# Moving lookup-table work of VectorE and ScalarE one place forward in the attention loop of a perceiver kernel

## The reference, cut to what matters

```python
kvx = jnp.einsum('bsi,oi->bso', cond, w_kv_x)
kx, vx = jnp.split(kvx, 2, axis=-1)
kx = _ln(kx.reshape(b, sc, g, d), kxln_w, kxln_b)
vx = vx.reshape(b, sc, g, d)
xout = _gqa(qx, kx, vx).reshape(b, s, nh * d)
```

```python
def _ghost_linear(x, idx, lut):
    w = lut[idx]
    return jnp.einsum('bsh,oh->bso', x, w)
```

## Time and profile before

| | us |
|---|---|
| median of 3 runs | 427.55 |
| lowest, highest | 427.23, 427.74 |
| profiled execution | 427.4 |
| its span, first to last instruction | 425.6 |
| TensorE (PE) busy | 414.7 |
| VectorE (DVE) busy | 347.2 |
| ScalarE (ACT) busy | 248.8 |
| GpSimd (POOL) busy | 35.8 |

### The profile page before, as it was taken

The page is one execution under the profiler, slowest core; times in us unless marked ns, Lnnn a source line. Parts: engine busy times, 40 slices in busy tenths (PEclk is TensorE's granted clock), DMA queues, the critical chain, the costliest instruction groups (busy, mean ns, idle before and its releaser), DMA issues.

```text
span 425.6 us, 6868 instructions
## 1 busy us (share of the span) xinstructions
PE 414.7 (97%) x2427; PEld 292.2 (69%) x2433; DVE 347.2 (82%) x699; ACT 248.8 (58%) x780; POOL 35.8 (8%) x58
## 2 busy tenths in 40 slices
PE   8999999999999999999999999999999999999897
PEld 3453455788885767778676686785486799837596
DVE  5889999987999899689899998978887787746831
ACT  2478898688547777748986677664505263220220
POOL 0010000040000001100001000010010004101000
PEclk9999999999999999999999999999999999999999
DMA  7599120500002015993554835688337979730000
GB/s 240 226 191 415 39 85 2 199 2 26 27 2 99 1 51 123 201 306 78 132 124 92 198 70 108 155 187 359 74 78 246 390 267 241 151 125 2 2 2 25
DMA packets 14591, 56.80 MB, mean 133 GB/s; under 512 B 1824, under 2 KB 2912, under 8 KB 13280
## 3 DMA queue, kind: packets, MB, share of 16 engines
q1 hardware_dynamic: 11104, 39.31, 25.3%
q0 software_dynamic: 3456, 17.11, 21.4%
HBM read 41.40 MB, written 0.26 MB: 98 GB/s over the span
## 4 chain that ended last, share of the span: by engine, by line
PE 74%; DVE 12%; issue 6%; DMA 4%; ACT 3%; POOL 1%; SPq 0%; DVEq 0%; ACTq 0%; POOLq 0%
PE PS L482 11%; PE PS L1817 10%; PE PS L453 8%; PE PS L454 8%; PE PS L455 8%; PE PS L1846 3%; PE PS L535 3%; PE PS L1287 3%; DMA lutw_dt.float<-luttmp_dt.float 2%; PE PS L1832 2%; DMA raw_dt.float<-in_wk_nat 1%; PE PS L492 1%; PE PS L1153 1%; PE PS L1135 1%; PE PS L1295 1%
## 5 line engine op out<-in xcount | busy, mean ns | idle before, releaser
L605 ACT ACTIVATE sq_dt.float<-PS 128x128 bf16<-128x128 f32 x256 | 67.0, 279 | 27.0 <-PE PS L455 20.5
L482 PE MATMUL PS<-s_dt.float,ctx_ring_dt.float 128*128 128x512 f32 x128 | 57.8, 593 | 0.0
L605 ACT ACTIVATION_READ_ACCUMULATOR sq_dt.float<-PS 128x1 f32 x256 | 53.6, 210 | 0.0
L453 PE MATMUL PS<-wkc_dt.float32r,ctx_hi_dt.float32r 128*128 128x512 f32 x128 | 51.5, 402 | 0.1
L454 PE MATMUL PS<-wkT_dt.float32r,ctx_hi_dt.float32r 128*128 128x512 f32 x128 | 50.0, 390 | 0.0
L455 PE MATMUL PS<-wkc_dt.float32r,ctxT_ring_dt.float32r 128*128 128x512 f32 x128 | 49.9, 390 | 0.0
L687 ACT ACTIVATE luttmp_dt.float<-low_bit_dt.float,vec_dt.float,small_dt.float 128x1536 f32<-128x1536 uint8 x24 | 38.5, 1654 | 8.5 <-DMA lutw_dt.float<-luttmp_dt.float 8.5
L1817 PE MATMUL PS<-wch_dt.float,xs_dt.float 128*128 128x512 f32 x96 | 42.0, 592 | 0.0
L482 PEld LDWEIGHTS PS<-s_dt.float,ctx_ring_dt.float 128*128 128x128 f32 x128 | 23.6, 190 | 23.6 <-issue 23.0
L700 POOL DMA_DIRECT2D lutw_dt.float<-luttmp_dt.float x21 | 18.2, 869 | 234.7 <-DVE luttmp_dt.float L694 234.7
L694 DVE SCALAR_TENSOR_TENSOR luttmp_dt.float<-idx_dt.float,luttmp_dt.float 128x1536 f32<-128x1536 uint8 x21 | 36.6, 1753 | 0.0
(11 more groups left out here) (304 smaller groups left out, 851.3 us busy)
## 6 DMA issues: line engine op xcount, KB each, us to landing
lutw_dt.float<-luttmp_dt.float POOLq DMA_DIRECT2D x21, 768.0 KB, 6.1
wch_dt.float<-in_chunks SPq DMA_DIRECT2D x5, 1024.0 KB, 7.9
ctxT_ring_dt.float<-in_ctxT SPq DMA_DIRECT2D x8, 512.0 KB, 3.4
ctx_ring_dt.float<-in_ctx SPq DMA_DIRECT2D x8, 512.0 KB, 3.9
keysT_dt.float<-in_ctxT SPq DMA_DIRECT2D x8, 512.0 KB, 7.0
keys_dt.float<-in_ctx SPq DMA_DIRECT2D x8, 512.0 KB, 8.0
zu_dt.float<-in_wproj SPq DMA_DIRECT2D x1, 2048.0 KB, 7.2
A_first_dt.float<-in_wproj SPq DMA_DIRECT2D x1, 2048.0 KB, 10.2
```

Of the source, the lines that this page charges most:

```text
L453: nc.tensor.matmul(o, x_hi, hi[:, c, :], start=c == 0, stop=False)
L482: last = nc.tensor.matmul(mix_bank(b, c), keysr[k][:, t, c * 128:c * 128 + 128], sS[k][:, t, :], start=t == 0, stop=t == KT - 1)
L605: last = nc.scalar.activation(sq[:, (4 * hf + g) * D:(4 * hf + g + 1) * D], key_bank(b, 2 * t + hf)[:, g * D:(g + 1) * D], ACT.Square, acc ...
```

## The change

A table `LUT_TERMS` now says which leaves and terms belong to which step. Step 1 has four, (0,0), (0,1), (0,2) and (1,0); step 2 has (1,1), (1,2), (2,0); step 3 has (2,1), (2,2), (3,0); step 4 has only (3,1) and (3,2); steps 5 to 7 are as they were. On ScalarE the first three of a step stand where the leaves stood, ahead of the inverse, and what is beyond three, which is (1,0) in step 1, stands behind the inverse and ahead of `split_context` and the squares. On VectorE the first and the second of a step stand where the first two terms stood, and the rest where the third stood. The order of the pieces, the helpers `leaf`, `term` and `add_terms`, their waits and the DMAs are unchanged.

```diff
--- before.py
+++ after.py
@@ -620,11 +620,12 @@
                     squares(1, 1, 0)
                 if more:
                     split_A(act, b + 1)
-                if b:
-                    for m in range(3):
-                        leaf(act, b - 1, m)
+                for place in LUT_TERMS[b][0:3]:
+                    leaf(act, *place)
                 if prev and more:
                     inverse(b - 1)
+                for place in LUT_TERMS[b][3:]:
+                    leaf(act, *place)
                 if next_context:
                     split_context(b + 2, k)
                 if more:
@@ -675,6 +676,13 @@
 
         LUT_STEPS = 6
 
+        LUT_TERMS = {b: [(b - 1, m) for m in range(3)] for b in range(5, 8)}
+        LUT_TERMS[0] = []
+        LUT_TERMS[1] = [(0, 0), (0, 1), (0, 2), (1, 0)]
+        LUT_TERMS[2] = [(1, 1), (1, 2), (2, 0)]
+        LUT_TERMS[3] = [(2, 1), (2, 2), (3, 0)]
+        LUT_TERMS[4] = [(3, 1), (3, 2)]
+
         def leaf(act, k, m):
 
 
@@ -767,7 +775,7 @@
                 maxima(b)
                 if b == 1:
                     lo_of_A(dve, 2)
-                term(dve, b - 1, 0)
+                term(dve, *LUT_TERMS[b][0])
                 shift(b, k)
                 normalise(b - 1, 1 - k)
                 if pair is not None:
@@ -777,11 +785,12 @@
                     lo_of_context(dve, b + 2, k)
                 if b == 4:
                     split_weights()
-                term(dve, b - 1, 1)
+                term(dve, *LUT_TERMS[b][1])
                 if pair is not None:
                     read_values(pair, 1)
                     quantize_values(pair, 1)
-                term(dve, b - 1, 2)
+                for place in LUT_TERMS[b][2:]:
+                    term(dve, *place)
                 if late_pair is not None:
                     for hf in range(2):
                         read_values(late_pair, hf)
```

## The result

The changed kernel takes 429.61 us (median of 9 runs, 428.02 to 431.25) against 427.54 us before (9 runs, 426.58 to 427.99): a ratio of 1.0052, 95% interval 1.0036 to 1.0068. It is slower by 2.1 us. The profiled execution took 429.53 us with a span of 427.7, 2.1 more than before. All its granted clock reads 1.00.

The account below looks back on a forecast made before the run. TensorE, busy 97% of the span, was taken to bound the kernel. From 427.4 us, +2.86 (step 1), -0.84 (step 4) and +1.37 (clock) gave 430.8, carried to the median 431.0 us; range 429.0 to 432.3.

Parts of the forecast that it names:

- The bound and the two excesses: TensorE, busy 97% of the span, bounds the kernel; steps 1 and 4 hold 0.80 and 0.84 us of waiting.
- Step 4, -0.84: One VectorE term fewer ahead of the key scale ends TensorE's wait at sequence 5's last score tile: -0.84 us.
- Step 1, +2.86: Leaf (1,0) on ScalarE waits for term (0,0), then runs, delaying split, squares and sequence 2's third key product: +2.86 us.
- The fourth term, steps 2 and 3, the DMAs, at nothing: Step 1's extra VectorE term lies in idle time; steps 2 and 3 wait for no accumulating DMA: 0 us.
- The clock, +1.37: TensorE's 3.1 us pause in step 1 exceeds 2.15 us, so the granted clock falls: +1.37 us.
- rival (a): Step 1's pause comes but the clock stays: 429.6 us, chance 0.40.
- the bound of two products, 2.74: Upper bound for the clock's cost after step 1's pause: two products at the low clock, 2.74 us.
- Rival (b): In step 1 other work covers the late squares' 2.86 us; only step 4's gain is left: 426.7 us, chance 0.05.
- (c): Part of step 1's delay is covered or taken back in steps 2 to 7: 427.9 us, chance 0.05.
- (d): Accumulating DMA lands after ScalarE reaches leaf (2,0) or (3,0): 433 us at 2 us, chance 0.04 with worse.

Follow-up runs that it names:

- the cause of step 4's taken out alone: Kernel before, with the last of four weight splits moved on VectorE from step 4 to step 5, no table work moved: 426.38 us against 427.44.
- both taken out: Kernel before, last weight split moved to step 5, three PSUM banks for sequence 2's keys, shift first in step 1: 425.53 us against 427.44.
- the longer pause: Changed kernel plus one 128x1536 activation on ScalarE in step 1 behind leaf (1,0): 432.44 us, ratio 1.0118.

## Why the prediction was right, and where it wasn't

**The bound and the two excesses** (0.80 us in step 1, 0.84 in step 4) were right: with the cause of step 4's taken out alone it is 24.97 us, and with both taken out step 1 is 24.98 and step 4 24.97. Step 1's was not taken out alone.

**Step 4, -0.84:** measured -0.85, and 25.83 again with the term back. The reason was VectorE's load, as the step said. The scaling was to start 0.8 us behind ScalarE's part of the scale; it did, at 231.64 behind 230.62 + 0.23 = 230.85.

**Step 1, +2.86:** measured +2.87. The context split starts 2.81 us later (136.75 to 139.56): 1.24 until the term was done (the wait shown is 1.17, predicted at about 1.2) and 1.57 for the leaf (1.59). The pause went from 0.28 to 3.1 us as predicted, and steps 2 to 7 took nothing of it back.

**The fourth term, steps 2 and 3, the DMAs, at nothing:** right. The three leaves of step 2 stand in one row from 157.00 without a gap, though the third now needs a DMA. The landings took 5.7 to 9.8 us.

**The clock, +1.37:** this step was wrong as a forecast of the median. I took one fall in the trace of before, 2.15 us after the last matmul, and a pause longer than that, and wrote the fall down as what happens. But 2.15 us was one draw, not a fixed delay: TensorE also stands still after the last matmul of every kernel here, and there the fall came 2.07 us after it in the profile with three terms in step 4, 3.5 in that with both excesses taken out, and 4.4 in that with a buffer of its own and the leaf ahead (the record of the clock reaches past the end of the span). In the changed kernel's first profile the clock was still at 1.00 when the span ended, 2.5 us after the last matmul. Its rows, and then those of the buffer of its own, leaf ahead:

```profile
422.39 2.76 PE L1304 MATMUL PS<-lutw_dt.float,ffn_dt.float 128*128 128x256 f32 x12
...
425.20:427.70 2.50, 0.00 (x0) 0.00 (x0) 0.41 (x1) 0.00 (x0) 0.00 (x0) 1.00 0.15 52
...
419.15 2.76 PE L1309 MATMUL PS<-lutw_dt.float,ffn_dt.float 128*128 128x256 f32 x12
...
422.00:426.30 4.30, 0.00 (x0) 0.00 (x0) 0.36 (x1) 0.00 (x0) 0.00 (x0) 1.00 0.09 32
426.30:426.40 0.10, 0.00 (x0) 0.00 (x0) 0.00 (x0) 0.00 (x0) 0.00 (x0) 0.73 0.00 0
```

The runs show that a pause of 3.1 us brings a fall in about half of the executions (8 of 15 of the changed kernel), and the median of a set depends on how many it holds: the first set, with 4 of 9, gave 429.61, the second, with 4 of 6, 430.86, and all 15 together 430.08. So that the result fell on rival (a)'s 429.6 is partly luck: the runs of that set without a fall have a median of 429.05, and the second set lies 0.1 below the forecast of 431.0. The chances (0.46 and 0.40) were about right, though I had meant them as doubt over one outcome, and not as its frequency. The price of a single fall was too small in the profile that shows one: 2.55 us, because the low level lasted 6.8 us, of which 5.96 held matmuls (142.97 to 148.93, 14 of them), more than two products of six and not one. The fall in the longer pause, with 4.28 us of matmuls at that level, cost some 1.9. Both stay within the bound of two products, 2.74. Between the medians of the two groups, 429.53 (7 runs at 1.00) and 430.88 (8 runs below), lie 1.35 us, much less than in that profile; a mean clock of 0.992 is that of the profile with 6.8 us at the low level, and 0.996, which four of the eight runs have, would be about half of that, an estimate.

By the Trainium skill, page "TensorE: Matmul & The Clock Gate", section "What's actually happening", idleness throttles and activity releases. These runs show both: the fall inside the pause and the return under load at 148.93. The size of the loss was left to the traces.

**Rival (b), the faster side,** is what happens when the leaf gets a buffer of its own and the place ahead of the inverse: 426.39 us was measured, where (b) had 426.7 for step 4's gain alone. The change as it is made never had that cover. Nothing showed for (c) and (d).

What stays open: where the falls of the 5 in 49 runs of the kernel before lie, since no profile caught one, why the same pause brings a fall in one execution and none in the next, and why the low level lasts longer in some runs.

## What to carry to other kernels

Before moving work of an engine that is "idle 40% of the time" forward, look at what is queued behind the new place: here a 1.6 us piece stood in front of the reads that free a two-bank PSUM ring, and the busiest engine had no slack there (it already waited 0.28 us and went on 0.06 us behind the last read), while the same piece, in a buffer of its own, fitted into 2.4 us of idle time ahead of the inverse. A buffer that is shared by successive pieces is also an ordering constraint; giving one piece its own took the loss of 2.1 us down to 0.6, which can't be told from no change, and the earlier place, which it makes possible, turned that into a gain of 1.0. The earlier place with the shared buffer was not run. And a pause of TensorE should be priced twice, once for its length and once, by the share of executions in which it comes, for the clock.

## What the runs showed of the hardware

- A pause of 1.9 us of TensorE brought the granted clock down in none of 12 runs; with one of 3.1 us it was low in 12 of 21, and with one of 4.7 us in 4 of 4. The two falls seen inside a pause came 2.26 and 2.12 us after the last matmul.
- The delay of a fall is not fixed: after the last matmul of the kernel it was 2.07, 2.15, 2.3, 3.5 and 4.4 us in five profiles (counted from the row's end, by which the two inside a pause are 2.10 and 1.96).
- After a fall inside the pause, in two profiles, the level of 1.2 GHz lasted 6.8 us (142.11 to 148.93; 140.29 to 147.12), well into full work, and cost 2.55 us in the first and some 1.9 in the second.
- Twelve matmuls on constants in a pause of 3.1 us held the clock in 11 of 12 runs; the time of the pause itself stayed.
